# First batch of a graph-attention kernel: value loads, label mask, edge terms, low parts of x and the values' product in another order

## The reference

```python
q_exp = where(x.sum(-1) == 0, 0, q[:, None, :])
self_feat = concat([x, q_exp]) @ W_self.T + b_self
output = self_feat
for d in range(2):
    A = adj if d == 0 else swapaxes(adj, 1, 2)
    A = A[:, :, :20, :]
    cond, vb = A.sum(-1), A @ w_bias + b_bias
    # attention: q from self_feat, k from its first 20 rows, 16 heads
    aff = where(cond > 0, q.k / sqrt(32), -9e15) + vb
    output += per_head(softmax(aff) @ kv, Wout[d]) + bout[d]
y = x + relu(output)
```

## Time and profile before

| what | value |
|---|---|
| median of 3 runs | 663.03 us (662.82 to 663.07) |
| the profiled execution | 662.91 us, its span 661.1 us |
| TensorE matmul busy | 640.3 us, 97% of the span |
| VectorE, ScalarE, GpSimd busy | 518.0, 386.9, 434.8 us |
| mean granted TensorE clock | 0.991 of 2.4 GHz |

### The profile page before, as it was taken

How to read it: one execution, slowest core, us unless ns; L and a number is a source line. 1 busy time by engine, 2 the same in 40 slices (tenths; PEclk the granted TensorE clock), 3 DMA queues, 4 the chain that set the end, 5 groups by cost and what they waited for, 6 DMA issues and landing times.

```text
span 661.1 us, 10066 instructions
## 1 busy us (share of the span) xinstructions
PE 640.3 (97%) x3802; PEld 559.0 (85%) x3802; DVE 518.0 (78%) x727; ACT 386.9 (59%) x705; POOL 434.8 (66%) x401
## 2 busy tenths in 40 slices
PE   9999995999999999999999999999999999999995
PEld 6877893898989897988889897998889898989793
DVE  4886775877888697978887797969797788867665
ACT  4635635856657474856576474857485665744433
POOL 0401366774979659775979478874977587966953
PEclk9999996999999999999999999999999999999999
DMA  9964423761849357553848275744857194835151
GB/s 363 390 240 125 141 84 126 174 238 53 218 150 237 101 115 261 130 186 72 278 103 263 49 178 188 176 164 90 275 92 234 55 236 133 236 107 113 49 138 64
DMA packets 53888, 109.51 MB, mean 166 GB/s; under 512 B 27791, under 2 KB 37775, under 8 KB 46863
## 3 DMA queue, kind: packets, MB, share of 16 engines
q1 hardware_dynamic: 51678, 93.13, 43.2%
q0 software_dynamic: 2160, 15.73, 13.2%
HBM read 88.05 MB, written 20.78 MB: 165 GB/s over the span
## 4 chain that ended last, share of the span: by engine, by line
PE 57%; DVE 21%; POOL 9%; ACT 8%; issue 3%; DMA 1%; SPq 1%; POOLq 0%; ACTq 0%
PE aff L497 19%; PE aff L477 11%; PE gen L444 5%; PE gen L446 5%; PE gen L445 5%; POOL z L1126 4%; DVE wtl L845 3%; DVE sff L831 3%; PE tp L507 3%; ACT wth L654 2%; ACT sfh L639 2%; POOL z L1138 2%; DVE bx L872 2%; DVE rsum L819 2%; DVE cond L876 2%
## 5 line engine op out<-in xcount | busy, mean ns | idle before, releaser
L497 PE MATMUL aff<-gh,sfl 128*128 128x320 f32 x512 | 116.7, 309 | 0.0
L497 PE MATMUL aff<-gl,sfh 128*128 128x320 f32 x512 | 116.6, 309 | 0.0
L497 PE MATMUL aff<-gh,sfh 128*128 128x320 f32 x512 | 116.6, 309 | 0.0
L444 PE MATMUL gen<-xh,w1h 128*128 128x512 f32 x256 | 105.8, 413 | 1.6 <-DVE sff L831 1.6
L1107 POOL TENSOR_TENSOR xl<-x,xh 128x512 fp32r<-128x512 f32 x62 | 84.2, 1403 | 34.3 <-ACT xh L621 34.3
L1114 POOL TENSOR_TENSOR z<-cb,bx 128x640 f32<-128x640 f32 x64 | 98.5, 1572 | 9.2 <-PE tp L446 9.2
L1111 POOL TENSOR_TENSOR sfl<-sff,sfh 128x512 fp32r<-128x512 f32 x48 | 61.3, 1288 | 64.7 <-ACT sfh L639 64.7
L445 PE MATMUL gen<-xl,w1h 128*128 128x512 f32 x256 | 101.7, 397 | 0.0
L446 PE MATMUL gen<-xh,w1l 128*128 128x512 f32 x256 | 101.6, 397 | 0.0
L771 ACT ACTIVATE z<-z 128x640 f32<-128x640 f32 x64 | 47.2, 738 | 89.3 <-POOL z L1126 89.3
L634 ACT ACTIVATE prod<-msk,wb 128x160 f32<-128x160 int32 x176 | 90.2, 587 | 5.3 <-DVE bx L872 3.4
(11 more groups left out here) (128 smaller groups left out, 1194.8 us busy)
## 6 DMA issues: line engine op xcount, KB each, us to landing
x<-in_x SPq DMA_DIRECT2D x16, 1024.0 KB, 8.5
xn<-in_xn SPq DMA_DIRECT2D x31, 512.0 KB, 5.4
sff<-in_x POOLq DMA_DIRECT2D x15, 1024.0 KB, 8.7
out_y<-sff SPq DMA_DIRECT2D x15, 1024.0 KB, 4.9
msk<-in_mask SPq DMA_DIRECT2D x17, 880.0 KB, 7.7
cb<-c_scratch SPq DMA_DIRECT2D x16, 320.0 KB, 6.9
nz<-nz_scratch SPq DMA_DIRECT2D x16, 256.0 KB, 3.4
wkT<-in_wkT SPq DMA_DIRECT2D x1, 2048.0 KB, 10.4
```

The lines of the kernel that those rows point to most:

```text
L444: nc.tensor.matmul(acc, lh, rh, start=first, stop=False)
L497: mm = nc.tensor.matmul(aff[:, t % 2, half, 0:SH], s, g[:, f, slot, half * SH:(half + 1) * SH], start=(f == 0 and i == 0), stop=(f == FC - ...
```

## The change

All edits are in the first batch, or just ahead of it; the work is the same, in another order.

- ScalarE: the third label group of batch 1 stands ahead of the batch; `edge_terms(1)` is behind exponential 0; the first label group of batch 2, with its waits for the mask and for both label sums of batch 1, is behind exponential 2 and so ahead of exponential 3; `sf_high(1, 1, 2)` goes behind the third group and `edge_terms(2)`.
- VectorE: the clearing of `va` is ahead of the batch; the two low parts of x stand behind shifts 0 and 1; label sums of batch 1 behind shift 3; the first row sums of batch 2 and `label_mask(2)` behind total 3; the second row sums of batch 2 and its flags (`nonzero`) behind `sf_low`.
- GpSimd: `value_rest(0)` moves behind all normalisations.
- SyncE's text is unchanged; what it waits for comes at other times.

```diff
--- before.py
+++ after.py
@@ -748,6 +748,7 @@
             act.wait_ge(s_sf, FC)
             x_high(1)
             labels(1, range(1, L, LG))
+            labels(1, range(2, L, LG))
 
             def batch(b, slot, i, ahead):
                 n, other = b + 1, 1 - slot
@@ -770,22 +771,19 @@
                         act.wait_ge(s_sub, b * T + (t + 1))
                     nc.scalar.activation(z[slot][:, t, :], z[slot][:, t, :], ACT.Exp).then_inc(s_exp, 1)
                     if b == 0 and t == 0:
-                        labels(1, range(2, L, LG))
-                    if b == 0 and t == 1:
                         edge_terms(1)
+                    if b == 0 and t == 2:
+                        act.wait_ge(s_mskin, 48)
+                        act.wait_ge(s_vred, 2 * D)
+                        labels(2, range(0, L, LG))
                     if ahead == 2 and b > 0 and t + 1 < LG:
                         labels(b + 2, range(t + 1, L, LG))
                     if ahead == 2 and b > 0 and t + 1 == LG:
                         edge_terms(b + 2)
                 if b == 0:
-
-                    act.wait_ge(s_mskin, 48)
-                    act.wait_ge(s_vred, 2 * D)
-                    labels(2, range(0, L, LG))
+                    labels(2, range(1, L, LG))
                     sf_high(1, 1, 0)
-                    labels(2, range(1, L, LG))
                     sf_high(1, 1, 1)
-                    sf_high(1, 1, 2)
                 for f in range(FC - 1):
                     if ahead >= 1 and b > 0:
                         sf_high(n, other, f)
@@ -797,6 +795,7 @@
                 if b == 0:
                     labels(2, range(2, L, LG))
                     edge_terms(2)
+                    sf_high(1, 1, 2)
                 if next_g:
                     evict_g(i + 1, GU - 2)
                     evict_g(i + 1, GU - 1)
@@ -1017,27 +1016,63 @@
             add_query(0, 0, 3)
             sf_low(0, 0)
             value_low(2, 1)
-            for c in range(XP, FC):
+            dve.wait_ge(s_vp, D * len(v_chunks))
+            nc.vector.memset(va[:].bitcast(F32), 0.0).then_inc(s_vz, 1)
+
+            def x_low(c):
                 dve.wait_ge(s_xh, FC + (c + 1))
                 nc.vector.tensor_tensor(xl[:, c, :], x[:, c, :], xh[:, c, :].bitcast(F32), ALU.subtract).then_inc(s_xl1, 1)
 
+            def first_batch(b, slot):
+                n, other = b + 1, 1 - slot
+                shift(b, slot, 0)
+                x_low(XP)
+                shift(b, slot, 1)
+                x_low(XP + 1)
+                total(b, slot, 0)
+                shift(b, slot, 2)
+                total(b, slot, 1)
+                shift(b, slot, 3)
+                dve.wait_ge(s_bx, T)
+                label_sum(n, 0)
+                label_sum(n, 1)
+                dve.wait_ge(s_out[other], 16)
+                add_query(n, other, 0)
+                total(b, slot, 2)
+                add_query(n, other, 1)
+                total(b, slot, 3)
+                row_sums(n + 1, 0, xn[:], s_xnin, 48)
+                label_mask(n + 1)
+                add_query(n, other, 2)
+                wt_low(b, slot, 0)
+                wt_low(b, slot, 1)
+                add_query(n, other, FC - 1)
+                wt_low(b, slot, 2)
+                wt_low(b, slot, 3)
+                add_sf(b, slot, 0)
+                wt_low(b, slot, 4)
+                add_sf(b, slot, 1)
+                sf_low(n, other)
+                row_sums(n + 1, 1, xn[:], s_xnin, 64)
+                nonzero(n + 1, True)
+                for j in range(2, HG):
+                    add_sf(b, slot, j)
+
             def batch(b, slot, i, ahead):
+                if b == 0:
+                    return first_batch(b, slot)
                 n, other = b + 1, 1 - slot
                 next_g = ahead >= 1 and slot == 1
-                if ahead >= 1 and b > 0:
+                if ahead >= 1:
                     dve.wait_ge(s_bx, b * T + T)
                     label_sum(n, 0)
                     label_sum(n, 1)
-                if ahead == 2 and b > 0:
+                if ahead == 2:
                     row_sums(b + 2, 0, xn[:], s_xnin, b * 32 + 48)
                 shift(b, slot, 0)
-                if ahead == 2 and b > 0:
+                if ahead == 2:
                     label_mask(b + 2)
                 shift(b, slot, 1)
-                if b == 0:
-                    dve.wait_ge(s_vp, D * len(v_chunks))
-                    nc.vector.memset(va[:].bitcast(F32), 0.0).then_inc(s_vz, 1)
-                    row_sums(2, 0, xn[:], s_xnin, 48)
                 total(b, slot, 0)
                 shift(b, slot, 2)
                 total(b, slot, 1)
@@ -1057,11 +1092,6 @@
                     dve.wait_ge(s_out[other], (i + slot) * 16 + 16)
                     add_query(n, other, 0)
                 total(b, slot, 3)
-                if b == 0:
-                    dve.wait_ge(s_bx, T)
-                    label_sum(1, 0)
-                    label_sum(1, 1)
-                    label_mask(2)
                 if next_g:
                     g_low(i + 1, 0)
                     g_low(i + 1, 1)
@@ -1184,7 +1214,8 @@
                 normalise(b, slot, 0)
                 sub_max(b, slot, 2)
                 normalise_rest(b, slot, 1)
-                value_rest(b)
+                if b > 0:
+                    value_rest(b)
                 normalise(b, slot, 1)
                 if ahead >= 1:
                     sub_max(b, slot, 3)
```

## The result

The changed kernel takes 655.02 us (median of 4, 654.63 to 655.30), the kernel before on the same chip 662.97 us: ratio 0.988, 95% interval 0.9863 to 0.9897. That is 7.95 us less.

A forecast was written before the change was run, and what follows sets the result against it. TensorE, busy 97%, was taken as the bound, with a hole in the first batch. Terms -10.4 + 3.4 + 0.8 = -6.2 us gave span 654.9 and time 656.8 us, range 653.6 to 660.0.

The forecast's parts named there:

- What bounds it, and the value loads: First batch: TensorE's hole comes from GpSimd's 5.50 us wait for value loads; mask load 5.8 earlier, wait gone.
- the list of signs: Trace observations named beforehand as showing the forecast right or wrong, such as batch 1 scores at 111, stall 2 to 4 us.
- The hole and what is late next: End of first batch: last exponential 97.9 to 98.6, last transpose 101.55, fourth self-feature block 102.1, TensorE standing about 1 us.
- ScalarE's chain: Label products of batch 2 to third weights eviction: starts 96.0, ends 106.7; batch 1 scores at 111.0, 10.4 us earlier.
- What the new order gives back: Batch 1 scores: later flags delay batch 3's row load to 119.4, VectorE's first shift waits, TensorE stands 3.4 us.
- my term: Time taken for batch 3's row load to land after issue: 5.4 us.
- The g low part: VectorE's g low part ahead of TensorE's next key products in batch 1: late with the row sums, TensorE loses 0.8 us.
- The row load in time (1): Batch 3's row load hides, bias sums bound next, stall only 0.5; gain 9 to 10, 654.0 to 653.0 us; chance 14%.
- The clock (2): TensorE's clock falls in the new stall inside batch 1 scores, losing 1.6 us; with slow landing 659.4 us; chance 19%.
- The mask (3): Batch 2's mask load stalls ScalarE's last exponential if landing exceeds 8.7 us; at worst 667.9 us; chance 4%, half slower.
- That the hole simply stays (4): Something other than value loads holds the first batch's hole: no change, 663 us; 3% together with the unforeseen.

The follow-up runs named there:

- two experiments: Changed kernel with, in batch 1, shift 0 ahead of the row sums and shift 1 ahead of the label mask, 653.86 us; changed kernel with batch 2's flags earlier, 653.73 us.
- the second execution: The changed kernel run once more, unaltered, in its profiled execution: 656.56 us; the median of that group was 655.44 us.
- the last experiment: Changed kernel with flags, shift 0 and self-feature sums moved earlier, plus batch 1's label mask behind shift 2 instead of shift 1: 653.02 us.
- the first experiment: Kernel before, with only GpSimd's product of the rest of the values moved behind the last normalisation: 657.23 us, ratio 0.9914.

## Why the prediction was right, step by step

- **What bounds it, and the value loads.** Right in the main. Mask load 87.12 (forecast 87.2), no wait of GpSimd. The value loads were slower than forecast: all issued by 94.25 (93.3, and 93.5 in the list of signs), since eight took 4.78 instead of 3.76, and in at 96.0 in the run with the old place of their product (94.8). It cost nothing, as their user stands last. What the prediction did not see is how the two halves of this step relate: the later user alone gives 5.8, the earlier loads alone 3.8, both 6.0.
- **The hole and what is late next.** Right within 0.2: label products at 96.06 (96.0), last exponential 98.00 (97.9), last weights' transpose 101.69 (101.55), fourth block 102.21 (102.1), TensorE standing 0.84 (about 1), and no fall of the clock there.
- **ScalarE's chain.** Right: eviction 106.74 (106.7), scores 110.98 (111.0).
- **What the new order gives back.** The mechanism was right and is shown by two experiments that take it away from opposite ends. The mis-sized term was the row load's arrival: forecast 119.4, measured 117.85. The flags took 0.29 (0.7 in the sum) and began 0.4 sooner; the landing took 4.7 (5.4). The stall was 1.9 against the due time instead of 3.4, and so just below the 2 to 4 in the list of signs. In the second execution the landing was 5.3, near my term, and the time 656.56.
- **A part of that was luck.** The low part ahead of the flags began at 110.64, just as one of GpSimd's bias sums ended, and took 0.68; the next bias sum took 2.07 instead of 1.57. With the flags early, the same low part began at 110.92, inside a bias sum, and took 1.90. Had it done so in the changed kernel, the row load would have come some 1.2 later, by my estimate from these rows, and the stall would have been near the forecast.
- **The g low part.** A further 0.8 was forecast. This term has a slip: with the row sums 5.7 earlier and 0.7 in hand (142.5 to 143.22), TensorE, 7.0 earlier at that point, loses 0.6, and the forecast should have read 656.6. The loss was 0.6, with the row sums 7.2 earlier and the same 0.7 in hand. So this term too followed the row load; the 1.55 of its arrival and the slip of 0.2 are the 1.8 by which the time lay below the forecast. Behind the row load the same wait hangs on the order of label mask and first total on VectorE, ahead of GpSimd's chain; it took the last experiment to name that member.
- **Rivals.** The row load in time (1) is what two variants made of it: 653.7 to 653.9, as its 653.0 to 654.0. The clock (2) fell in one execution, for 656.6. The mask (3) landed after 6.0 of the 8.7 us that it had; issued 5.0 us later on purpose, it cost at most some 0.5, which the times do not tell from nothing. That the hole simply stays (4) is out by the first experiment: with the product of the values last, and nothing else, 5.8 of it went.

Left open is why the landing of the same 512 KB row load moves between 3.9 and 5.3 us in the six traces that issue it at 113 to 115. Its issue alone took between 0.62 and 1.29, and a longer issue went with a longer landing (0.62 and 3.9, 1.01 and 4.7, 1.29 and 5.3). GpSimd's own DMA that adds x is issued about 2 us behind it. That this transfer makes the landing long is not borne out: in the three traces that issue the load at 108.1, 6 to 7 us ahead of that transfer, the issue took 0.44 to 0.45 and the landing 5.4 to 6.4.

## What to carry to other kernels

When a wait is taken out of an order written by hand, work out the whole next pass of each queue that depends on the moved steps: here flags moved 10 us towards their user pushed one load on SyncE past its due time, and a fifth of the gain was lost. Two cures for one wait (load earlier, use later) do not add up; try the cheaper one alone first. A short stall that hangs on a transfer varies with it, from 0.9 to 2.3 us in the five traces that have it, and behind the longest of them TensorE's clock fell too.

## What the runs showed of the hardware that was not expected

VectorE's instructions with two inputs in SBUF and GpSimd's hold each other up, and by how much depends on which starts first. In the changed kernel, the two low parts of x on VectorE, then GpSimd's subtraction that met the first:

```profile
83.20 0.68 DVE L1024 TENSOR_TENSOR xl<-x,xh 128x512 fp32r<-128x512 f32 x1
...
86.72 1.64 DVE L1024 TENSOR_TENSOR xl<-x,xh 128x512 fp32r<-128x512 f32 x1
```
```profile
83.36 1.65 POOL L1156 TENSOR_TENSOR z<-z,mx 128x640 f32<-128x640 f32 x1 [0.46 <-DVE mx L883]
```

The same operation takes 0.68 when it starts with GpSimd idle and 1.64 when it starts inside an instruction of GpSimd; GpSimd's subtraction, 1.28 elsewhere, takes 1.65 when it starts inside VectorE's. It is the start that counts, and not that GpSimd is busy over the whole stretch. The last low part of the self features meets GpSimd's four bias sums in both of these rows, first in the changed kernel, between two sums, then with the flags early, inside one:

```profile
110.64 0.68 DVE L835 TENSOR_TENSOR sfl<-sff,sfh 128x512 fp32r<-128x512 f32 x1
```
```profile
110.92 1.90 DVE L835 TENSOR_TENSOR sfl<-sff,sfh 128x512 fp32r<-128x512 f32 x1
```

The sum of self features at 108.56, with one input in PSUM, takes 0.68 inside a bias sum. So a short operation with two inputs in SBUF costs by what runs beside it: the flags took 0.16, 0.29, 0.49 and 1.20 in these traces.
